# First sums of a two-layer graph network on one core: where two-piece float32r products begin, block 28 or block 21

## The chip, the cores and the metric

One core of a Trainium2 chip. The metric is the device time of one execution in microseconds (us), lower is better; the median of three executions of the kernel before is 3544.65 us.

## The reference, cut to what matters

6,250 nodes with 128 features, 200,000 edges sorted by destination. `h` is the layer norm of `x` followed by relu. Layer 0 (SAGE) needs for each node the mean of `h` over its incoming edges:

```python
msgs = h[src]
summed = jax.ops.segment_sum(msgs, dst, num_segments=N_NODES)
cnt = jax.ops.segment_sum(jnp.ones_like(dst, dtype=h.dtype), dst, num_segments=N_NODES)
return summed / jnp.maximum(cnt, 1.0)[:, None]
```

Two dense products, a residual and a layer norm follow; then comes layer 1, graph attention with four heads over the same edges, whose sums are done later in the kernel. Only the building of `summed` of layer 0 is touched here.

## The kernel before, in words

The kernel runs in stages one behind the other; `stage()` ends each with a barrier. The change concerns two of them.

**front** normalises `x` into `H`, finds where each node's edges start, and splits every row of `H` into pieces whose sum is the float32 value. The 49 blocks of 128 nodes are handled in seven groups of seven (`residual`, `lowest`, `second`, L487 to L668). Groups below `C_BF` = 28 become three bf16 pieces in `SPL`; the others become two pieces with 12 bits masked off, `CPR`, of type float32r. Between the groups ScalarE and TensorE also work through 26 steps of the edge attributes (`more(2)`).

**count_sums** computes the sums without fetching a row per edge. For each of 62 tiles (49 tiles of up to 128 edges per node, "pair tiles", and 13 tiles of the edges that did not fit, "odd tiles") it counts how often each source node occurs for each of 128 destinations, and multiplies this matrix of counts with the pieces of `H`. A tile of counts is made in eight units (u = 0 to 7) of 16 destinations:

- VectorE writes one-hot rows for two units at a time, `OHL` and `OHH` (`one_hots`, L1082), into a ring of three. It may start entry m when TensorE has used entry m-3 (`s_bm`). In an odd tile `OHL` is twice as long. It also adds up the pieces of a finished tile (`rows`, L1101) and prepares the next tiles' keys; its first one-hots of a tile need `LH`, which ScalarE turns at unit 2 of the tile before (L930).
- TensorE multiplies the one-hots of a unit into PSUM (`counts`, L981). `psA` has two places, so `counts` of unit n waits until unit n-2 has been copied.
- ScalarE copies each unit from PSUM into the bf16 matrix of counts `A[i % 2]` (L948).

The product of tile i-1 with the pieces is put between the counts of tile i: after `counts(i, u)`, for u of 1 and up, TensorE does `product(i - 1, range(7 * u - 7, 7 * u))`, seven blocks. A block h below `C_BF` takes the bf16 counts as weights and streams three pieces, 384 columns (L992). A block from `C_BF` on takes counts in float32r (`AR`) and streams two pieces, 256 columns (L998). ScalarE casts them, seven blocks a time (`cast`, L933 to L938), in the unit that `C_AT` names, behind that unit's copy:

```python
if u == 2 and i + 1 < NSL and of[i + 1] > of[i]:
    turned(of[i + 1])
if i >= 1 and u in C_AT:
    if u == C_AT[0]:
        act.wait_ge(s_ev, UNITS * i)
    cast(i - 1, C_AT.index(u))
```

So before the change block groups 28 to 34, 35 to 41 and 42 to 48 are multiplied in units 5, 6 and 7 and cast in units 1, 3 and 5. TensorE waits for cast g at the first block of its group (L997). The last tile has no tile behind it: all its casts and products are done at the end (L956 to L958 and the last call of `product`).

The order of the tiles is fixed: 14 pair tiles, then two pair tiles and two odd tiles in turn until the 13 odd ones are done, then pair tiles alone. GpSimd fetches the sources of each pair of tiles with an indirect DMA (L896), and ahead of that scatters 49 times into `s_tab` (L910), on which the edge lists of the odd tiles rest.

`OHH` and `AR` lie over tables that only later stages fill: `AR` begins at `tables_at`, and `OHH` behind its `C_FR` blocks.

Of the kernel before, what the change touches and what calls it, by code (L numbers as in the profile page):

```python
# [34 lines left out]
N_BLK = -(-N_NODES // P)  # L35
# [45 lines left out]
NV = N_BLK * P  # L81


C_BF, C_FR = 28, N_BLK - 28
C_CAST = [range(28, 35), range(35, 42), range(42, 49)]
C_AT = (1, 3, 5)
assert C_BF % 7 == 0 and C_FR == 7 * len(C_CAST)
PAST_ROW = 256.0
assert 2 * N_BLK <= P and PAST_ROW == 2 * P
# [51 lines left out]
def build(nc, x, src, dst, edge_attr, W1l, W1r, b1, W2l, W2r, b2, gamma, beta,  # L141
          W, W_edge, att_src, att_dst, att_edge, bias, out):
    with ExitStack() as top:
# [623 lines left out]
        def count_sums(at, block):  # L767
# [157 lines left out]
            def _(act):  # L925
                def turned(f):
                    act.wait_ge(s_tt, f + 1)
                    if f >= 2:
                        act.wait_ge(s_oh, UNITS // 2 * (last[f - 2] + 1))
                    act.copy(LH[:, f % 2], psT[:, 0:2 * P].rearrange("p (n c) -> p n c", n=2)[:, :, :, None]  # L930
                             .to_broadcast([P, 2, P, 2])).then_inc(s_lh, 1)

                def cast(i, g):  # L933
                    rows_ = C_CAST[g]
                    if i >= 1:
                        act.wait_ge(s_cu, len(C_CAST) * (i - 1) + g + 1)
                    act.copy(AR[:, rows_[0] - C_BF:rows_[-1] + 1 - C_BF], A[i % 2][:, rows_[0]:rows_[-1] + 1]
                             ).then_inc(s_cs, 1)  # L938

                turned(0)  # L940
                for i in range(NSL):
                    for u in range(UNITS):
                        n = UNITS * i + u
                        act.wait_ge(s_bm, n + 1)
                        if u == 0 and i >= 2:
                            act.wait_ge(s_cu, len(C_CAST) * (i - 1))
                            act.wait_ge(s_sv[i % 2], 16 * (i // 2))
                        act.copy(A[i % 2][:, :, UN_S * u:UN_S * (u + 1)].rearrange("p h (k s) -> p k h s", k=2),  # L948
                                 psA[:, n % 2, :, 0:W8].rearrange("p k (s h) -> p k h s", s=8)).then_inc(s_ev, 1)
# [6 lines that stand above are left out]
                act.wait_ge(s_ev, UNITS * NSL)  # L956
                for g in range(len(C_CAST)):
                    cast(NSL - 1, g)  # L958

            @block.tensor  # L960
            def _(pe):
# [23 lines left out]
                def product(i, rows):  # L985
# [4 lines left out]
                    for h in rows:  # L990
# [4 lines left out]
                        g = (h - C_BF) // 7  # L995
                        if h == C_CAST[g][0]:
                            pe.wait_ge(s_cs, len(C_CAST) * i + g + 1)  # L997
# [1631 lines left out]
```

## Time and profile before

| | before |
|---|---|
| runs (us) | 3544.65, 3550.16, 3542.03; median 3544.65 |
| the profiled execution | 3543.3 us, its span 3541.5 us |
| mean granted TensorE clock over the span | 0.803 |
| TensorE busy / its weight loads | 82% / 70% of the span |
| VectorE / ScalarE / GpSimd busy | 72% / 39% / 55% |
| stage count_sums | from about 125 us to 829 us of the span |

Start times in rows of the timeline are us from the start of the span. A timeline row merges neighbouring instructions of one line: `x7` are seven. The bracket at its end tells how long the engine had been idle before it and what released it. In rows of PEld (weight loads) a seven of L992 or L998 is one product of seven blocks, and the row of L981 before it is the counts of one unit (eight loads in a pair tile, sixteen in an odd one). A name such as `AE` for `A` is the profile's: the counts lie in the memory of tensor `AE`.

### The profile page before, as it was taken

The page shows a single profiled execution, that of the slowest core. Times are in us where ns is not written, and L with a number is a line of the kernel's source. Part 1 is how long each engine was busy: PE and PEld are TensorE (multiplying, and loading weights), DVE is VectorE, ACT ScalarE, POOL GpSimd, SP SyncE. Part 2 cuts the span into 40 slices and gives each one's busy share as a digit, 9 for nine tenths or more (in the row PEclk, how much of TensorE's full clock was granted, in tenths as well). Part 3 has the DMA queues.
Part 4 walks back from the last instruction along what each step waited for, and adds up shares of the span by engine and source line. Part 5 has one row for each costly group of instructions (what it writes and reads, how often), then busy time and mean ns, then how long its engine had stood idle before and what let it go on. Part 6 is the DMA issues. An engine that isn't in the chain of part 4 may idle for free. (4 is left out here: it accounts for less than half of the span.)

```text
span 3541.5 us, 66684 instructions
## 1 busy us (share of the span) xinstructions
PE 2894.2 (82%) x21816; PEld 2493.7 (70%) x21816; DVE 2558.1 (72%) x6864; ACT 1382.8 (39%) x2754; POOL 1941.0 (55%) x1972
## 2 busy tenths in 40 slices
PE   5789999999998999797777777777777777777774
PEld 5667777888877777587666766766666676676663
DVE  4779999995576765587666766766666676676667
ACT  4578777885445566322212222221221222222120
POOL 5430111251013332477777777777777777777773
PEclk9999999999999999676666666666666666666666
DMA  5233333582379888322222222222222222222225
GB/s 170 102 139 151 135 154 149 166 192 92 112 251 257 269 248 261 114 55 56 55 55 55 55 55 55 55 55 55 55 56 54 56 55 55 55 55 55 55 55 97
DMA packets 150470, 378.35 MB, mean 107 GB/s; under 512 B 39080, under 2 KB 87776, under 8 KB 141780
## 3 DMA queue, kind: packets, MB, share of 16 engines
q0 software_dynamic: 66640, 129.84, 17.4%
q1 hardware_dynamic: 42120, 217.23, 16.5%
q10 hardware_dynamic: 41372, 26.95, 2.6%
q8 instruction: 191, 3.13, 0.4%
q14 instruction: 147, 1.20, 0.1%
HBM read 255.78 MB, written 119.69 MB: 106 GB/s over the span
## 5 line engine op out<-in xcount | busy, mean ns | idle before, releaser
L2165 POOL DMA_INDIRECT G<-x_tab,idx x1611 | 1530.5, 950 | 490.8 <-issue 490.8
L2255 PE MATMUL pu<-MSG,OH 128*128 128x140 f32 x3282 | 627.0, 353 | 1.4 <-DVE ACC L2352 1.3
L2186 ACT COPY OHT<-pt 128x512 f32<-128x512 f32 (+1 forms) x432 | 236.5, 558 | 974.3 <-PE pt L2231 972.8
L2352 DVE TENSOR_TENSOR ACC<-pu,ACC 128x140 f32 x1641 | 485.1, 296 | 139.7 <-PE pu L2255 93.5
L2255 PEld LDWEIGHTS pu<-MSG,OH 128*128 128x128 f32 x3282 | 560.3, 247 | 4.8 <-DVE ACC L2352 1.4
L2244 PE MATMUL px<-ADG,OHT 128*128 128x4 f32 x3240 | 468.4, 271 | 0.0
L948 ACT CAST AE<-psA 128x784 bf16<-128x784 f32 x496 | 397.5, 815 | 139.2 <-PE psA L981 138.4
L2244 PEld LDWEIGHTS px<-ADG,OHT 128*128 128x128 f32 x3240 | 440.4, 213 | 10.4
L2277 PE MATMUL pc<-ident,L 128*60 128x128 f32 x108 | 42.3, 391 | 447.2 <-DVE L L2420 447.2
L1082 DVE TENSOR_TENSOR OHL<-iol,LH 128x2048 bf16<-128x2048 bf16 (+1 forms) x248 | 358.3, 1445 | 22.3 <-PE psA L981 16.2
L2231 PE MATMUL pt<-ident,OH 128*128 128x128 f32 x1620 | 354.9, 379 | 11.9 <-ACT OHT L2186 10.7
L2277 PEld LDWEIGHTS pc<-ident,L 128*60 128x60 f32 x108 | 13.6, 126 | 480.0 <-issue 480.0
L992 PE MATMUL psR<-SPL,AE 128*128 128x384 bf16 x1736 | 324.0, 327 | 0.0
L2231 PEld LDWEIGHTS pt<-ident,OH 128*128 128x128 f32 x1620 | 281.5, 200 | 60.2 <-ACT OHT L2186 35.1
L1627 ACT CAST AR<-AE 128x896 fp32r<-128x896 bf16 x248 | 246.0, 1017 | 163.8 <-PE psR L1816 107.8
L1816 PE MATMUL psR<-SPR,AR 128*128 128x256 f32 x1922 | 291.2, 297 | 15.2 <-ACT AR L1627 15.0
L2413 DVE TENSOR_TENSOR L<-G,AE 128x60 f32<-128x60 f32 x108 | 27.9, 258 | 350.4 <-DMA G<-x_tab,idx 350.3
L981 PE MATMUL psA<-OHH_c,OHL 128*128 128x98 bf16 (+1 forms) x4800 | 259.8, 201 | 22.9 <-DVE OHH_c L1082 22.5
L1816 PEld LDWEIGHTS psR<-SPR,AR 128*128 128x128 f32 x1922 | 253.0, 194 | 29.7 <-ACT AR L1627 20.0
L981 PEld LDWEIGHTS psA<-OHH_c,OHL 128*128 128x128 bf16 x4800 | 219.1, 98 | 71.6 <-DVE OHH_c L1082 35.6
L896 POOL DMA_INDIRECT srows<-src_pad,EKI x38 | 65.7, 1729 | 350.7 <-DVE KB L1064 194.5
L2323 DVE TENSOR_TENSOR MSG<-G,pq 128x1920 f32<-128x1920 f32 (+1 forms) x109 | 231.6, 2125 | 17.3 <-issue 17.3
(427 smaller groups left out, 4532.6 us busy)
## 6 DMA issues: line engine op xcount, KB each, us to landing
a_tab<-AE SPq DMA_DIRECT2D x62, 1568.0 KB, 5.7
AE<-a_tab SPq DMA_DIRECT2D x60, 800.0 KB, 5.6
AE<-a_tab SPq DMA_DIRECT2D x60, 768.0 KB, 7.0
G<-x_tab,idx POOLq DMA_INDIRECT x1611
at_in<-in_edge_attr SPq DMA_DIRECT2D x26, 250.0 KB
SUMS<-in_edge_attr ACTq DMA_DIRECT2D x24, 250.0 KB
ae_t<-room ACTq DMA_DIRECT2D x13, 256.0 KB, 7.0
AE<-ae_t SPq DMA_DIRECT2D x1, 3328.0 KB, 11.9
```

What stands on the lines that cost most here:

```text
L948: act.copy(A[i % 2][:, :, UN_S * u:UN_S * (u + 1)].rearrange("p h (k s) -> p k h s", k=2), psA[:, n % 2, :, 0:W8].rearrange("p k (s h) -> ...
L981: mm = pe.matmul(psA[:, n % 2, c * w // W8, to:to + w], OHL[:, m % RING, k], OHH[:, m % RING, k * step:k * step + w], start=True, stop=True)
L992: pe.matmul(psR[:, i % 2, 0:3 * D], A[i % 2][:, h, :], SPL[:, h].rearrange("p s f -> p (s f)"), start=(h == 0), stop=False)
L1082: return dve.tensor_tensor(out.rearrange("p (s h t) -> p s h t", s=k, t=2), columns[:, 0:w].rearrange("p (h t) -> p h t", t=2)[:, None].to ...
L1627: act.copy(AR[:, n % 3, 0:len(rows_)], A[i % 2][:, rows_[0]:rows_[-1] + 1]).then_inc(s_cs, 1)
L1816: mm = pe.matmul(psR[:, i % 2, 0:2 * D], AR[:, n % 3, k], SPR[:, h - N_BF].rearrange("p s f -> p (s f)"), start=False, stop=(h == N_BLK - 1))
L2165: pool.indirect_dma_start(G[:, u % 4, j, :], None, x_tab, bass.IndirectOffsetOnAxis(ap=idx[:, u % 4, j:j + 1], axis=0)).then_inc(s_g[u % 4 ...
L2186: act.copy(OHT[:, 4 * n:4 * n + w, :].rearrange("p a b -> p (a b)"), pt[:, n % 2, 0:w * P]).then_inc(s_te, 1)
L2231: mm = pe.transpose(pt[:, n % 2, (j % 4) * P:(j % 4 + 1) * P], OH[:, u % 4, j, :], ident[:])
L2244: mm = pe.matmul(px_l[:, :, j], OHT[:, j, :], ADG[:, j, :], start=True, stop=True)
L2255: mm = pe.matmul(pu[:, k[0], k[1]:k[1] + MW], OH[:, u % 4, j, :], MSG[:, u % 2, j, :], start=True, stop=True)
L2352: dve.tensor_tensor(a, pu[:, k[0], k[1]:k[1] + MW][:, None, :], a, ALU.add).then_inc(s_c, 1)
```

## The change

Three constants. The fourth group of seven blocks, 21 to 27, goes from three bf16 pieces to two float32r pieces; it is multiplied in unit 4. There are four casts a tile instead of three, and they stand in units 1, 2, 4 and 6.

```diff
-C_BF, C_FR = 28, N_BLK - 28
-C_CAST = [range(28, 35), range(35, 42), range(42, 49)]
-C_AT = (1, 3, 5)
+C_BF, C_FR = 21, N_BLK - 21
+C_CAST = [range(21, 28), range(28, 35), range(35, 42), range(42, 49)]
+C_AT = (1, 2, 4, 6)
```

With `C_BF` and `C_FR` the sizes of `SPL`, `CPR` and `AR` change, and the place of `OHH`. In front, the group 21 to 27 is now split as groups 28 to 48 are: `residual` masks bits instead of subtracting, and the cast of L507 into `SPL` falls away.

## Rows read from the trace of the kernel before

**Rows 1.** Busy time by stretch: us, then PE, PEld, DVE, ACT, POOL, PEclk, DMA share, GB/s
```profile
225.00:301.00 76.00, 76.00 (x831) 61.16 (x830) 70.85 (x101) 62.89 (x82) 6.22 (x5) 1.00 0.38 154
330.00:600.00 270.00, 253.99 (x3416) 201.06 (x3412) 268.82 (x315) 209.85 (x272) 42.46 (x17) 1.00 0.37 145
610.00:820.00 210.00, 210.00 (x2342) 170.13 (x2340) 192.64 (x236) 180.73 (x236) 71.12 (x55) 1.00 0.67 173
```
**Rows 2.** Waits, 300 to 600 us: waiter, releaser, us in total, times, longest
```profile
PE psA L981 <- DVE OHH_c L1082: 17.0, 21, 1.8
DVE OHL L1082 <- PE psA L981: 0.4, 1, 0.4
```
**Rows 3.** Waits, 600 to 830 us
```profile
DVE OHL L1082 <- PE psA L981: 8.9, 16, 0.7
```
**Rows 4.** Timeline of the weight loads, one pair tile: start us, us, engine, line
```profile
708.53 0.74 PEld L981 LDWEIGHTS psA<-OHH_c,OHL 128*128 128x128 bf16 x16
...
713.24 0.53 PEld L981 LDWEIGHTS psA<-OHH_c,OHL 128*128 128x128 bf16 x8
...
714.73 0.53 PEld L981 LDWEIGHTS psA<-OHH_c,OHL 128*128 128x128 bf16 x8
...
716.15 0.39 PEld L981 LDWEIGHTS psA<-OHH_c,OHL 128*128 128x128 bf16 x8
...
717.43 0.38 PEld L981 LDWEIGHTS psA<-OHH_c,OHL 128*128 128x128 bf16 x8
717.76 0.89 PEld L998 LDWEIGHTS psR<-CPR,AR_c 128*128 128x128 f32 x7
718.69 0.75 PEld L981 LDWEIGHTS psA<-OHH_c,OHL 128*128 128x128 bf16 x16
```
**Rows 5.** Timeline of ScalarE in units 5 to 7 of the same tile
```profile
715.46 0.81 ACT L948 CAST AE<-psA 128x784 bf16<-128x784 f32 x1 [0.63 <-PE psA L981]
716.16 0.95 ACT L937 CAST AR_c<-AE 128x896 fp32r<-128x896 bf16 x1
717.00 0.81 ACT L948 CAST AE<-psA 128x784 bf16<-128x784 f32 x1
718.00 0.81 ACT L948 CAST AE<-psA 128x784 bf16<-128x784 f32 x1 [0.18 <-PE psA L981]
```
**Rows 6.** Timeline at the end of the stage, last copy and bf16 products
```profile
820.28 0.81 ACT L948 CAST AE<-psA 128x784 bf16<-128x784 f32 x1 [0.18 <-PE psA L981]
...
821.14 4.34 PEld L992 LDWEIGHTS psR<-SPL,AE 128*128 128x128 bf16 x28 [0.21 <-ACT AE L948]
```
**Rows 7.** Timeline of VectorE where the first stretch of the stage ends
```profile
214.24 0.24 DVE L1056 TENSOR_SCALAR lo_i<-srows 128x128 int32<-128x128 int32 x1 [14.88 <-DMA srows<-src_pad,EKI]
```
**Rows 8.** Timeline of VectorE, last one-hots ahead of the odd tiles
```profile
301.22 1.23 DVE L1082 TENSOR_TENSOR OHL<-iol,LH 128x2048 bf16<-128x2048 bf16 x1 [0.44 <-PE psA L981]
...
306.16 2.29 DVE L1082 TENSOR_TENSOR OHL<-iol,LH 128x4096 bf16<-128x4096 bf16 x1 [0.34 <-ACT LH L930]
```
**Rows 9.** Timeline among the odd tiles: a counts load and the one-hot that needs it
```profile
445.35 0.53 PEld L981 LDWEIGHTS psA<-OHH_c,OHL 128*128 128x128 bf16 x8
...
447.71 2.29 DVE L1082 TENSOR_TENSOR OHL<-iol,LH 128x4096 bf16<-128x4096 bf16 x1
```
**Rows 10.** Timeline of the weight loads, last wait for one-hots in the stage
```profile
603.12 0.47 PEld L981 LDWEIGHTS psA<-OHH_c,OHL 128*128 128x128 bf16 x16 [0.73 <-DVE OHH_c L1082]
```
**Rows 11.** VectorE's sums of finished tiles, grouped by line, 228 to 304 us
```profile
L1101 DVE TENSOR_REDUCE SUMS<-psR 128x128 f32<-128x384 f32 x8 | 4.4, 547 | 0.0
```
**Rows 12.** The same, 606 to 822 us
```profile
L1101 DVE TENSOR_REDUCE SUMS<-psR 128x128 f32<-128x384 f32 x21 | 11.6, 552 | 6.5 <-PE psR L998 6.5
L1101 DVE TENSOR_REDUCE R<-psR 128x128 f32<-128x384 f32 x1 | 0.5, 549 | 0.0
```
**Rows 13.** Timeline of VectorE in front, the lowest pieces of blocks 21 to 27
```profile
91.39 1.09 DVE L665 TENSOR_TENSOR SPL<-SUMS,SPL 128x896 bf16<-128x896 f32 x1 [2.50 <-ACT SPL L490]
```

**Rows 14.** Weight loads of this line, 300 to 600 us: busy us, mean ns of one
```profile
L998 PEld LDWEIGHTS psR<-CPR,AR_c 128*128 128x128 f32 x538 | 68.8, 189 | 0.0
```

## The prediction

> **What bounds the kernel now.** I read the busy time by stretch first, since the change acts only while the first sums are built (about 130 to 829 us) and a little before. In the pair tiles ahead of and behind the odd ones TensorE is busy 76.00 of 76 us and 210.00 of 210; between 330 and 600 us it is VectorE, 268.82 of 270 [rows 1]. The waits say the same from the other side: among the odd tiles TensorE waits 17.0 us for one-hots, in 21 waits, and VectorE 0.4 us for TensorE [rows 2]; behind them VectorE waits 8.9 us for TensorE [rows 3], and TensorE's last wait for one-hots is at 603 us [rows 10]. So a microsecond of TensorE counts in pair tiles and is covered among odd ones.
>
> The pace of a pair tile is in its weight loads. A tile takes 718.69 - 708.53 = 10.16 us. A unit whose counts and product both follow bf16 work takes 714.73 - 713.24 = 1.49 us, the unit in which float32r begins 716.15 - 714.73 = 1.42, and a unit after that (718.69 - 716.15) / 2 = 1.27 [rows 4].
>
> Beside it runs ScalarE. It starts a copy 718.00 - 717.43 = 0.57 us after the first load of the counts (behind a float32r group), a cast 716.16 - 715.46 = 0.70 us after the copy, the next copy 717.00 - 716.16 = 0.84 us after the cast, and the cast takes 0.95 [rows 4, 5]. From the end of a copy to the load that waited for it pass 821.14 - (820.28 + 0.81) = 0.05 us [rows 6]. No row shows TensorE waiting for a cast of this stage now.
>
> **The change, part by part.**
>
> *Products.* Unit 4 turns from bf16 into float32r: one unit of 1.49 us goes, one of 1.27 comes, -0.22 us per pair tile.
>
> *The fourth cast.* Its duration isn't the question, its place is. Casts in units 1, 2 and 4 are early enough: the groups are needed in units 4, 5 and 6, and the tightest, cast in unit 4, ends about 0.73 + 0.70 + 0.95 = 2.4 us after the first load of that unit's counts (0.73 = 715.46 - 714.73), while its group is due two units later, after 1.42 + 1.27 + 0.33 = 3.0 us (0.33 from the counts' load to the group's, 717.76 - 717.43). The last cast stands in unit 6 and its group in unit 7. From the first load of unit 6's counts it can be there after 0.57 (copy may start) + 0.70 (cast starts) + 0.95 (cast done) + 0.05 (handed over) = 2.27 us. TensorE wants it after one unit and the counts of unit 7: 1.27 + 0.33 = 1.60 us [rows 4, 5, 6]. So TensorE waits 2.27 - 1.60 = 0.67 us in every tile. Before the change that cast stood a unit earlier and had 1.27 us more.
>
> Is ScalarE free by then? Behind the cast of unit 4 the copy of unit 5 starts at 0.73 + 0.70 + 0.84 = 2.27 us after unit 4's first load, instead of 1.42 + 0.57 = 1.99, and is over its 0.70 at 2.97; the copy of unit 6 can't start before 1.42 + 1.27 + 0.57 = 3.26. So the lateness does not add up. Its whole tile is 8 x 0.70 + 4 x 0.84 = 9.0 us and, every other tile, one turning of keys, under the new tile. What is queued behind the late cast is the copy of unit 7; it starts 0.57 + 0.70 + 0.84 = 2.11 us after unit 6's first load instead of 1.27 + 0.57 = 1.84, and the next counts come after the waiting product, later still. Nobody else waits for it.
>
> Net per pair tile in which TensorE sets the pace: +0.67 - 0.22 = **+0.45 us**, 10.61 for 10.16. VectorE's tile is at most 192.64 x 10.16 / 210 = 9.3 us of work there [rows 1], and stays covered.
>
> *How many tiles count.* Three parts:
> - Up to 214 us nothing: VectorE waits 14.88 us for an indirect DMA of sources, which stands on GpSimd behind its 49 scatters [rows 7]; the six or so tiles ahead of it, 0.45 us later each, fit into that.
> - From there to the odd tiles TensorE leads: 8 tiles are summed up between 228 and 304 us [rows 11]. The lateness goes over to VectorE by its last waits for TensorE's counts and for the turned keys, 0.44 us at 301.22 and 0.34 at 306.16 [rows 8]. 8 x 0.45 = +3.6 us.
> - Among the odd tiles VectorE leads. Does TensorE's lateness reach it through the ring of three? Two pair tiles in a row make TensorE at most 0.67 + 2 x 0.45 = 1.6 us late before VectorE's next long stretch. The tightest use that I find there: the one-hot at 447.71 needs counts loaded from 445.35, finished at about 445.35 + 0.73 = 446.1, 1.6 us before [rows 9]; at that point the lateness is 0.67 + 0.45 = 1.1 us. It holds, with 0.5 us to spare: 0 us.
> - After the last wait for one-hots at 603.12 [rows 10] TensorE leads to the end: 21 + 1 = 22 tiles [rows 12]. One of them carries the small merging products between counts and product of unit 6, which give the cast the time; I count 21: 21 x 0.45 = +9.4 us.
>
> *The end of the stage.* The last tile's products stand alone. Its seven blocks change their type too: -0.2 us as above. The 0.21 us that its first load waits for the last copy [rows 6] falls into the lateness: -0.2. The four casts run beside the first 21 blocks: these take 21 x 4.34 / 28 = 3.3 us, the cast needed first 0.95, each further one 0.84.
>
> *Front.* ScalarE loses one cast of seven blocks (0.95 us in count_sums [rows 5]), and the lowest piece of blocks 21 to 27 no longer waits 2.50 us for a copy of ScalarE's [rows 13]. The gain lies between 0 (the edge attributes' steps beside it are the pace) and 2.5 us. VectorE's next but one step waits for ScalarE's relu anyway, so only a part of that cast can come through: I take -0.5.
>
> Memory: the last table is written after the stage; no transfer is added. Each tile has one instruction more on ScalarE and one wait more on TensorE.
>
> **The sum.** 3.6 + 9.4 - 0.4 - 0.5 = +12.1 us. The profiled execution goes from 3543.3 to 3555.4 us. It lies 1.35 under the median of the runs, so in their terms 3544.65 + 12.1 = **3556.8 us**, 0.34% slower.
>
> **One rule against the trace.** Seven float32r loads are done within 0.89 us [rows 4] though one alone takes 189 ns [rows 14], which seven times over is 1.32: the loads overlap the matmuls and each other. The Trainium skill, "TensorE: Matmul & The Clock Gate", section "The mechanism", has it that a weight load overlaps matmuls in flight only when they use other rows of the array; by that rule the new group would cost its loads in full. The trace does not agree.
>
> **Rivals.**
> 1. *The wait isn't there and the saving is* (faster). TensorE would take up other work of its queue while the late group waits, the next tile's counts, so that only -0.22 is left. On 8 + 21 tiles that is -6.4, with -0.4 and -0.5 more about 3537 us. For it: all casts arrive in time now. Against it: the four durations above, and TensorE's waits for one-hots [rows 2], in which it did nothing else. It decides at 2.27 against 1.60 us. 7%.
> 2. *Covered* (no change). VectorE, 92% busy from 610 us on [rows 1], sets the pace more than I think, or the wait is 0.4 instead of 0.67: then +0.15 or so per tile, +4 us, 3549. For it: VectorE is close behind. Against it: it waits 16 times for TensorE [rows 3]. 11%.
> 3. *The odd tiles give way too* (slower still). If the 0.5 us to spare in the ring is less than nothing, each of the six rounds of two pair and two odd tiles loses up to 1 us: +6, 3563. 6%.
> 4. *The clock falls* (slower still). TensorE's waits of up to 1.8 us among the odd tiles leave the granted clock at 1.00 [rows 1, 2], that is 2.4 GHz, so 0.67 us a tile should too. If it spent 3% of 290 us at 1.2 GHz: about +9, 3565. The Trainium skill, "TensorE: Matmul & The Clock Gate", section "A second HAM failure mode: psum-queue depth-cycling", tells of frequent short idles between groups of matmuls that make the clock swing; the trace does not agree so far. 3%.
> 5. *Serial loads* (slower still). The new group's loads take 1.32 us instead of the 1.27 - 0.33 = 0.94 of its product now: +0.38 per tile, +11 us, 3568. Seven loads in 0.89 us speak against it. 1%. This is the rule of the section "The mechanism" as a mechanism.
>
> **How the numbers follow.** My forecast gets 72%: the wait rests on four measured durations, and the number of tiles on two counts. Its own range is 3549 to 3564 (0.35 to 0.55 net per tile, front 0 to -2.5, and the runs before spread from 3542 to 3550). A measurement of this kernel tells about 0.2%, 7 us, from no change, so slower means above 3551.7. Slower: forecast, 3, 4 and 5, 0.82. The same: 2, 0.11. Faster: 1, 0.07. The range of 3548 to 3565 takes in the forecast and rival 3.
>
> **What would show it.** In the profile after: a wait of the L998 loads for the cast of L937 of about 0.67 us, once a tile, in unit 7, up to 60 times (there is none now); tiles of 10.6 us behind the odd ones; four casts of 0.95 us; float32r sevens at 0.89; rounds of tiles among the odd ones as long as before; the wait at 214 us shorter. Wrong would be tiles of 9.94 us (rival 1), or VectorE waiting among the odd tiles (rival 3).

## The result, and the profile after

| | before | after |
|---|---|---|
| median of the runs, us | 3546.22 (3542.03 to 3556.97, 7 runs) | 3562.20 (3557.37 to 3569.17, 7 runs) |
| profiled execution, us (span) | 3543.3 (3541.5) | 3560.56 (3558.7) |
| ratio after to before | | 1.0040, 95% interval 1.0027 to 1.0053 |

The change makes the kernel slower by 0.40%, 14 us (10 to 19); the two medians themselves lie 16.0 us apart. Forecast were +12.1 us and 3556.8 us; the range of 3548 to 3565 holds the median.

The wait that the forecast rests on is there. First the waits of TensorE for this cast over the whole program, then those of 300 to 600 us and of 600 to 830 us, in the kernel after (waiter, releaser, us in total, times, longest):

```profile
PEld psR L998 <- ACT AR_c L937: 30.7, 61, 0.6
```
```profile
PEld psA L981 <- DVE OHH_c L1082: 21.3, 22, 2.1
PE psA L981 <- DVE OHH_c L1082: 15.6, 17, 1.8
PEld psR L998 <- ACT AR_c L937: 9.6, 26, 0.6
DVE OHL L1082 <- PE psA L981: 0.4, 1, 0.4
```
```profile
DVE OHL L1082 <- PE psA L981: 11.5, 22, 0.7
DVE OHL L1082 <- ACT LH L930: 7.2, 9, 1.0
```

Before, L998 waited for no cast. Now it waits 61 times: once in each tile that has a product between its counts, 0.62 us in pair tiles that TensorE leads, 0.16 to 0.5 us among the odd ones. Among the odd tiles VectorE's waits for TensorE are as before (0.4 us, once [rows 2]); behind them they grew from 8.9 us in 16 to 11.5 in 22 [rows 3], and those for the turned keys from 2.3 to 7.2.

In one pair tile behind the odd ones, first the weight loads of units 4 to 7, then ScalarE beside them (start us, us, engine, line; to be held against [rows 4, 5]):

```profile
721.27 0.53 PEld L981 LDWEIGHTS psA<-OHH_c,OHL 128*128 128x128 bf16 x8
721.75 0.90 PEld L998 LDWEIGHTS psR<-CPR,AR_c 128*128 128x128 f32 x7
722.68 0.39 PEld L981 LDWEIGHTS psA<-OHH_c,OHL 128*128 128x128 bf16 x8
723.02 0.89 PEld L998 LDWEIGHTS psR<-CPR,AR_c 128*128 128x128 f32 x7
723.95 0.38 PEld L981 LDWEIGHTS psA<-OHH_c,OHL 128*128 128x128 bf16 x8
724.28 0.89 PEld L998 LDWEIGHTS psR<-CPR,AR_c 128*128 128x128 f32 x7
725.22 0.39 PEld L981 LDWEIGHTS psA<-OHH_c,OHL 128*128 128x128 bf16 x8
726.23 0.89 PEld L998 LDWEIGHTS psR<-CPR,AR_c 128*128 128x128 f32 x7 [0.62 <-ACT AR_c L937]
727.17 0.75 PEld L981 LDWEIGHTS psA<-OHH_c,OHL 128*128 128x128 bf16 x16
```
```profile
724.53 0.81 ACT L948 CAST AE<-psA 128x784 bf16<-128x784 f32 x1 [0.17 <-PE psA L981]
725.24 0.94 ACT L937 CAST AR_c<-AE 128x896 fp32r<-128x896 bf16 x1
726.08 0.82 ACT L948 CAST AE<-psA 128x784 bf16<-128x784 f32 x1
```

Units 5 and 6 take 1.27 us each (counts at 722.68, 723.95, 725.22), and in unit 7 the last group's loads stand still. Unit 6 starts at 723.95; its copy starts at 724.53, the cast at 725.24, ends at 726.18, and the load comes at 726.23: 2.28 us after the unit's start, where the forecast had 2.27. Of the 2.28 - 1.60 = 0.68 us the row shows 0.62 as idle; the rest is the overlap with the counts' loads that is lost (a group that doesn't wait starts 0.33 us after the counts' first load, while those loads take 0.38).

Over seventeen pair tiles behind the odd ones, a tile takes 10.68 us (sums of finished tiles, L1101, from 642.44 to 823.94) where it took 10.23 (638.21 to 812.14): +0.45, as forecast. The 10.16 of the prediction is one tile of that row, a little shorter than the mean.

VectorE's sums of finished tiles mark the stage's stretches, before and after:

```profile
219.35 0.55 DVE L1101 TENSOR_REDUCE SUMS<-psR 128x128 f32<-128x384 f32 x1
330.99 0.55 DVE L1101 TENSOR_REDUCE SUMS<-psR 128x128 f32<-128x384 f32 x1
599.42 0.55 DVE L1101 TENSOR_REDUCE SUMS<-psR 128x128 f32<-128x384 f32 x1
828.42 0.56 DVE L1101 TENSOR_REDUCE SUMS<-psR 128x128 f32<-128x384 f32 x1 [6.68 <-PE psR L998]
```
```profile
219.38 0.55 DVE L1101 TENSOR_REDUCE SUMS<-psR 128x128 f32<-128x384 f32 x1
334.45 0.55 DVE L1101 TENSOR_REDUCE SUMS<-psR 128x128 f32<-128x384 f32 x1
602.85 0.55 DVE L1101 TENSOR_REDUCE SUMS<-psR 128x128 f32<-128x384 f32 x1
840.89 0.56 DVE L1101 TENSOR_REDUCE SUMS<-psR 128x128 f32<-128x384 f32 x1 [6.23 <-PE psR L998]
```

| stretch | before | after | difference | forecast |
|---|---|---|---|---|
| from the gap for the sources to VectorE's lead | 111.64 | 115.07 | +3.43 | +3.6 |
| odd tiles in turn | 268.43 | 268.40 | 0 | 0 |
| to the last sum | 229.00 | 238.04 | +9.04 | +9.4 - 0.4 |
| together | 609.07 | 621.51 | +12.44 | +12.6 |

The granted clock was 1.00 in the windows of 225 to 300, 330 to 600 and 640 to 800 us, as before.

### The profile page after: what moved, and what is told of

It is laid out like the page before. It is cut to its first block and busy times, and to the rows that moved or that the text cites. A ratio compares the mean times of both kernels' runs of the same rounds, so it can differ in the third digit from the quotient of the medians.

```text
span 3558.7 us, 66745 instructions
## 1 busy us (share of the span) xinstructions
PE 2887.6 (81%) x21816; PEld 2508.1 (70%) x21816; DVE 2555.3 (72%) x6864; ACT 1426.0 (40%) x2815; POOL 1936.4 (54%) x1972
## 5 line engine op out<-in xcount | busy, mean ns | idle before, releaser
L2244 PEld LDWEIGHTS px<-ADG,OHT 128*128 128x128 f32 x3240 | 442.6, 214 | 10.4
L998 PE MATMUL psR<-CPR,AR_c 128*128 128x256 f32 x1736 | 267.4, 293 | 22.0 <-ACT AR_c L937 21.8
```

What stands on the lines that cost most here:

```text
L998: mm = pe.matmul(psR[:, i % 2, 0:2 * D], AR[:, h - C_BF], CPR[:, h - C_BF].rearrange("p s f -> p (s f)"), start=False, stop=(h == N_BLK - 1))
L2244: mm = pe.matmul(px_l[:, :, j], OHT[:, j, :], ADG[:, j, :], start=True, stop=True)
```

## The experiments

My theory: the time is lost at the place of the last cast, and the fourth float32r group by itself is worth 0.22 us a pair tile. The edits are against the kernel after unless they say otherwise. All of them are read by the same stretch, from the sum behind the gap at about 219 us to the last sum, which was 609.07 us before and 621.51 after.

### The last two casts one unit earlier each

```diff
-C_AT = (1, 2, 4, 6)
+C_AT = (1, 2, 3, 5)
```

> The change with its casts in units 1, 2, 3 and 5 instead of 1, 2, 4 and 6. Theory A (the place of the last cast costs): the wait of about 0.62 us a tile goes and only the cheaper unit is left, -0.22 us on 8 + 21 tiles and -0.4 at the end, so 6 to 7 us under the kernel before (ratio 0.998), tiles of about 10.0 us behind the odd ones. Rival B (the fourth cast costs as work of ScalarE, wherever it stands): as slow as the change, ratio 1.004. Rival C (float32r blocks cost TensorE more than bf16 ones): slower than before too, with sevens longer than 0.94 us.

Measured: 3538.97 us against 3547.11 of the kernel before in the same set, ratio 0.9976 (0.9964 to 0.9988). It beats both kernels. L998 waits for no cast. The seventeen tiles behind the odd ones take 10.02 us each (636.18 to 806.53). One pair tile, weight loads, then ScalarE:

```profile
741.48 0.89 PEld L998 LDWEIGHTS psR<-CPR,AR_c 128*128 128x128 f32 x7
742.41 0.38 PEld L981 LDWEIGHTS psA<-OHH_c,OHL 128*128 128x128 bf16 x8
742.74 0.89 PEld L998 LDWEIGHTS psR<-CPR,AR_c 128*128 128x128 f32 x7
743.68 0.38 PEld L981 LDWEIGHTS psA<-OHH_c,OHL 128*128 128x128 bf16 x8
744.01 0.89 PEld L998 LDWEIGHTS psR<-CPR,AR_c 128*128 128x128 f32 x7
```
```profile
738.91 0.97 ACT L937 CAST AR_c<-AE 128x896 fp32r<-128x896 bf16 x1
739.75 0.84 ACT L948 CAST AE<-psA 128x784 bf16<-128x784 f32 x1
740.45 0.98 ACT L937 CAST AR_c<-AE 128x896 fp32r<-128x896 bf16 x1
741.30 1.56 ACT L948 CAST AE<-psA 128x784 bf16<-128x784 f32 x2
742.70 1.00 ACT L937 CAST AR_c<-AE 128x896 fp32r<-128x896 bf16 x1
```

The last group is loaded at 744.01, 0.31 us after its cast ended at 743.70. ScalarE works in this part of the tile without a pause, but TensorE doesn't feel it: its busy time is 75.00 of 75 us and 159.94 of 160 in the windows of 225 to 300 and 640 to 800 us. The stretch takes 603.03 us (219.25 to 822.28), 6.0 less than before; 29 tiles at 0.22 are 6.4, and with the end of the stage 6.8 had been expected. So the change's first part is the gain that the forecast put into it, and the places of the casts turned it into a loss; the next run moves the last one alone.

### The last two casts in units 4 and 5

```diff
-C_AT = (1, 2, 4, 6)
+C_AT = (1, 2, 4, 5)
```

> The change with its casts in units 1, 2, 4 and 5. Theory A: the last cast ends about 3.97 us after the first load of unit 4's counts and is wanted at 4.29, so it is in time by 0.3 us: as fast as with casts in 1, 2, 3 and 5, 6 to 7 us under the kernel before. Rival B: two casts in neighbouring units of 1.27 us make ScalarE late and cost some tenths a tile, ratio 1.000 to 1.004. Rival C: slower than before.

Measured: 3542.61 us, ratio 0.9979 (0.9965 to 0.9993). No wait for a cast; the stretch takes 602.65 us (217.81 to 820.46). This is the single move from unit 6 to 5, with the other three casts where the change has them. It gives back 18.9 us of the stretch, 29 tiles at 0.65, which is the forecast's 0.67. The two placings can't be told apart in time.

### The kernel before with its last cast in unit 6

Against the kernel before:

```diff
-C_AT = (1, 3, 5)
+C_AT = (1, 3, 6)
```

> The kernel before with its three casts in units 1, 3 and 6 instead of 1, 3 and 5: no fourth cast, no further float32r block. Theory A: a wait of 0.62 to 0.67 us a tile and nothing saved, on 8 + 21 tiles: +18 to +19 us, ratio 1.005; nothing lost among the odd tiles (lateness 1.3 us against 1.6). Rivals B and C: nothing changes, ratio 1.000, since ScalarE's work and the blocks are the same.

Measured: 3569.52 us, ratio 1.0068 (1.0049 to 1.0087), about +24 us (17 to 31). Its stretch grew by 19.9 us (218.76 to 847.74 is 628.98), where 18 to 19 were expected; the 4 us more in the ratio are within its interval. Seventeen tiles take 10.90 us each (644.96 to 830.29), 0.67 more than before. The waits of 600 to 830 us in it:

```profile
DVE OHL L1082 <- PE psA L981: 15.6, 27, 0.7
PEld psR L998 <- ACT AR_c L937: 12.4, 21, 0.6
```

With three groups and no fourth cast the same wait is there, once a tile and 0.6 us long in these. So neither the number of casts nor ScalarE's load makes it; the place alone does. Wait without saving costs 19.9, saving without wait brings 6.0 to 6.4, both together 12.4: the parts add up to within 1.5 us.

### The last cast in unit 7

```diff
-C_AT = (1, 2, 4, 6)
+C_AT = (1, 2, 4, 7)
```

> The change with its casts in units 1, 2, 4 and 7, a unit later still. Theory A: the wait is 0.57 + 0.70 + 0.95 + 0.05 - 0.33 = 1.94 us a tile, net 1.72 on 29 tiles: +50 us; and now the lateness at the tightest one-hot among the odd tiles, 3.7 us, is over the 1.6 that it can hide, so VectorE waits there up to 2 us in each of six rounds: +50 to +62 us in all, ratio 1.014 to 1.018. If the slack among the odd tiles is larger than I read it: +50. Rivals B and C: as slow as the change, +14.

Measured: 3683.12 us, ratio 1.0377 (1.0352 to 1.0401): far above what the wait alone would give. The stretch takes 740.49 us (220.96 to 961.45), 131 more than before; VectorE no longer waits at the gap at 214 us. The wait has the length that was worked out; what comes behind it was not expected. Weight loads at the end of a pair tile, then TensorE's matmuls, then the busy time of the window and of a quiet one (us, PE, PEld, DVE, ACT, POOL, granted clock, DMA share, GB/s):

```profile
806.88 0.89 PEld L998 LDWEIGHTS psR<-CPR,AR_c 128*128 128x128 f32 x7 [1.89 <-ACT AR_c L937]
...
809.16 0.15 PEld L992 LDWEIGHTS psR<-SPL,AE 128*128 128x128 bf16 x1 [0.17 <-issue]
809.48 0.15 PEld L992 LDWEIGHTS psR<-SPL,AE 128*128 128x128 bf16 x1 [0.17 <-issue]
...
813.26 0.95 PEld L992 LDWEIGHTS psR<-SPL,AE 128*128 128x128 bf16 x7
```
```profile
806.89 1.10 PE L998 MATMUL psR<-CPR,AR_c 128*128 128x256 f32 x7 [1.74 <-ACT AR_c L937]
...
808.84 2.45 PE L992 MATMUL psR<-SPL,AE 128*128 128x384 bf16 x7
```
```profile
808.00:812.00 4.00, 4.00 (x35) 2.73 (x33) 2.67 (x3) 2.39 (x4) 3.39 (x3) 0.57 1.06 275
816.00:820.00 4.00, 2.80 (x36) 2.54 (x32) 3.72 (x4) 3.35 (x5) 0.74 (x1) 1.00 0.13 11
```

Between 808 and 812 us the granted clock is 0.57, that is 1.2 GHz for most of the window, and the loads start 0.32 us apart. Seven of them at 2.4 GHz are done in 0.95 us (813.26). Before the clock fell the engine had stood still for 1.74 us, as it does once in every tile. Seven tiles from 713.10 to 808.02 take 13.56 us each, 3.33 more than the 10.23 of before: 1.89 - 0.22 = 1.67 is the wait less the saving, and the other 1.66 is what the slow stretch costs.

The wait alone does not settle it, though. It stands in the last tiles of the stage as well, 1.89 us once a tile, and there the clock stays up:

```profile
848.00:960.00 112.00, 96.34 (x1048) 79.82 (x1047) 81.25 (x97) 89.66 (x116) 34.17 (x25) 1.00 0.63 152
```

Nine tiles from 847.20 to 954.66 take 11.94 us each, 1.71 more than 10.23: the wait less the saving, and nothing for the clock. What keeps it up there no run shows.

And the odd tiles give way here. VectorE's waits from 330 to 700 us:

```profile
DVE OHL L1082 <- PE psA L981: 37.8, 41, 2.2
```

It was 0.4 us, once, in both kernels [rows 2]. The lateness of TensorE is now over what the ring of three has to spare: the rounds of two pair and two odd tiles take 54 to 56 us instead of 47.05, and the stretch of the odd tiles 313.11 us (361.83 to 674.94) instead of 268.43. It is the prediction's rival 3, at a lateness that this change doesn't reach.

The Trainium skill, "TensorE: Matmul & The Clock Gate", section "A second HAM failure mode: psum-queue depth-cycling", tells of short idles between groups of matmuls that make the clock swing. With idles of 1.74 us once a tile this trace agrees up to 825 us, and not behind that; with idles of 0.5 us once a tile (the kernel after) it does not.

### Does the clock need the fourth group, too?

Two kernels ran on another chip, on which the program takes some 1180 us longer, the kernel before included (4728.19 us there). With float32r from block 35 on, which ran on both chips, this stage starts 44 us later there (170.4 for 126.7) and its last sum comes 79 us later (918.50 for 839.03); the rest of the time is lost behind it. Only comparisons within that set count. Against the kernel before:

```diff
-C_AT = (1, 3, 5)
+C_AT = (1, 3, 7)
```

> The kernel before with its casts in units 1, 3 and 7. If the clock is what I missed with the last cast in unit 7 of the change: waits of 1.9 us a tile, behind each a stretch of 3.4 us at 1.2 GHz that costs 1.7 us, so 3.6 us on each pair tile (13.8 instead of 10.2), granted clock 0.88 to 0.91 in the stage, rounds of two pair and two odd tiles of some 54 to 55 us instead of 47: +140 us, ratio 1.039 to 1.041. If the excess came with the fourth group or the cast of unit 4 beside it instead, and the wait costs only its own length: 1.9 us on 29 tiles and up to 2 us in each of six rounds, +55 to +67 us, ratio 1.016 to 1.019, clock 1.00.

Measured: 4882.88 us, ratio 1.0335 (1.0312 to 1.0358), that is +158 us. Its windows:

```profile
330.00:600.00 270.00, 234.65 (x2757) 186.58 (x2755) 225.66 (x270) 181.18 (x232) 30.52 (x16) 0.93 0.30 122
640.00:800.00 160.00, 140.13 (x1687) 111.10 (x1688) 134.10 (x155) 106.70 (x138) 17.17 (x7) 0.91 0.32 128
```

With three groups the clock falls as well, and the loss is nearer to the +140 of the theory with the clock than to the +55 to 67 without. So the fall needs neither the fourth group nor the cast of unit 4. The 18 us over the 140 can be found in the sums of finished tiles. On that chip the gap for the sources lies behind the sum of the second tile and not of the fifth, so three more tiles count, 3 x 3.6 = 11 us; and the odd tiles take 312.9 us (439.55 to 752.47), 44.5 more than before, where the forecast left them 140 - 29 x 3.6 = 36. From the gap to the last sum pass 807.04 us (259.38 to 1066.42), and in the next kernel, on the same chip, 657.00 (261.50 to 918.50); that one is 32 x 0.22 = 7 us slower than the kernel before, so the stretch grew by about 157 us of the 158.

### Float32r from block 35 on

The other direction: 14 blocks in float32r, two casts, the last still in unit 5.

```diff
-C_BF, C_FR = 21, N_BLK - 21
-C_CAST = [range(21, 28), range(28, 35), range(35, 42), range(42, 49)]
-C_AT = (1, 2, 4, 6)
+C_BF, C_FR = 35, N_BLK - 35
+C_CAST = [range(35, 42), range(42, 49)]
+C_AT = (3, 5)
```

> The other way: only blocks 35 to 48 in float32r, two casts in units 3 and 5, products in units 6 and 7; one float32r group fewer than the kernel before. Theory A: every cast is in time (no wait of an L998 load), and one unit of 1.27 us turns back into 1.49: +0.22 us on 8 + 21 tiles and +0.2 at the end, 6 to 7 us over the kernel before, ratio 1.0018; the stage from the 14 us gap to its end is 6 us longer. Rival B (a cast costs as work of ScalarE): a cast fewer makes it faster than before, by 12 us if one cast more costs that. Rival C (float32r costs TensorE more): faster too.

Measured on that other chip: 4741.68 us, ratio 1.0026 (1.0012 to 1.0040), with a single wait for a cast, 0.15 us just behind the gap, and pair tiles of 10.4 to 10.5 us. It ran again on a chip like that of the first sets, with a profile of the kernel before beside it:

> The kernel before once more, for its profile on the chip of this set. All theories: no difference from the kernel before; its tiles behind the odd ones are the measure for the next run: 10.2 us.

> Blocks 35 to 48 alone in float32r, two casts in units 3 and 5, again, since the first time it came out at twice what Theory A says (+12 us against 6 to 7) on a chip that was 1180 us slower in the later stages. Theory A: the stage from its sources gap to its end 6 to 7 us longer than the kernel before, tiles behind the odd ones 10.4 to 10.5 us, ratio 1.0018. Rivals B and C (a cast, or a float32r group, costs more than it gives): shorter stage, ratio under 1.

Measured: 3549.61 us for 3546.69 of the kernel before in the same set, ratio 1.0020 (1.0006 to 1.0035); the profiled execution of the kernel before took 3544.35. The stretch takes 609.33 us in the first (218.57 to 827.90), 615.74 in the second (223.29 to 839.03): +6.4. The float32r group adds or saves the same in both directions, 6.0 to 6.4 us for 29 tiles, with ScalarE loaded less or more. So what a group gives or costs shows on TensorE alone.

What wasn't tried: a fifth group (float32r from block 14 on). `OHH`, which lies behind `AR`, would then reach into `rowi`, a small table that is filled earlier and read later, so the two would have to be placed anew. ScalarE's round would be 8 x 0.70 + 5 x 0.84 = 9.8 us and every other tile a turning of keys (0.48 to the next instruction, 738.43 to 738.91 in the first experiment), against 10.23 - 2 x 0.22 = 9.8 of TensorE: whether the gain goes on is open.

## Why the prediction was right

*What bounds.* Right. TensorE was busy 75.00 of 75 us where the last cast was early enough, and each change of its work came through in full in the pair tiles ahead of and behind the odd ones. Among the odd ones it did not come through at all, up to the lateness of this change; with the last cast in unit 7 it did.

*The product, -0.22 a pair tile.* Right: -6.0 and -6.4 us over 29 tiles alone, and +6.4 the other way. Three groups in a row at 1.27 us a unit, seven loads in 0.89 us each, speak once more against the rule of the Trainium skill ("TensorE: Matmul & The Clock Gate", section "The mechanism") that loads overlap matmuls only with other rows of the array. The same section also names a background weight buffer, into which a load may go ahead of matmuls in flight; these traces agree with that, and can't show the buffer.

*The late cast, +0.67.* Right: 2.28 us for 2.27, and 29 x 0.65 when the cast is moved back. Four durations, read where the same instructions already stood, gave a wait that no row of before showed.

*The number of tiles, 8 and 21.* Right to within 0.2 us in both stretches (+3.43 for +3.6, +9.04 for +9.0). One tile behind the odd ones waits only 0.16 us instead of 0.62 (at 630 us), as the prediction had it for the one with the merging products.

*The end of the stage, -0.4.* Right: from the last sum but one to the last pass 6.79 us (834.10 to 840.89) for 7.24 (821.18 to 828.42).

*The odd tiles, 0.* Right: 268.40 us for 268.43. The spare of 0.5 us held; unit 7's cast, with a lateness far over it, shows that there is such a limit.

*Who else waits: nobody.* Right for the time, incomplete as a list. The turned keys, which ScalarE writes in unit 2, reach VectorE later: its waits for them grew by 4.9 us behind the odd tiles. TensorE set the pace there anyway, and they lie beside its lateness, as the +9.04 shows. One of them stands ahead of the odd tiles, 1.01 us where [rows 8] have 0.34 at 306.16:

```profile
309.62 2.29 DVE L1082 TENSOR_TENSOR OHL<-iol,LH 128x4096 bf16<-128x4096 bf16 x1 [1.01 <-ACT LH L930]
```

*Front, -0.5, and the gap.* Wrong, and by my own argument. The same wait of VectorE in the kernel after:

```profile
214.28 0.23 DVE L1056 TENSOR_SCALAR lo_i<-srows 128x128 int32<-128x128 int32 x1 [15.26 <-DMA srows<-src_pad,EKI]
```

I had it shorter; it is 0.38 us longer than 14.88 [rows 7]. Both ends have to be counted from the stage's start (VectorE's first instruction of it, L1154, at 124.77 before and 122.65 after). From there the last one-hots ahead of the gap start at 75.40 us for 73.62, so the tiles were late by 1.8 us, and this lateness the gap swallowed, as forecast. But the gap also ended later, 91.63 us behind the start for 89.47. GpSimd's scatters begin with the stage and ended 1.6 us earlier than before (206.63 for 208.22); then GpSimd waited 4.22 us for them to land, for 2.51 before, and the fetch behind them was issued at 211.74 for 211.61.

So the 2.1 us by which the stage began earlier were lost in this pair, and nothing of the -0.5 can be in the +12.44. That is no rule: over the seven profiled executions in which the gap ends between 212 and 219 us, it ends 89.4 to 91.6 us behind the stage's start, and the latest start, 126.70, has the latest end. This is the run with float32r from block 35 on:

```profile
218.20 0.23 DVE L1056 TENSOR_SCALAR lo_i<-srows 128x128 int32<-128x128 int32 x1 [16.07 <-DMA srows<-src_pad,EKI]
```

What moves the stage's start moves the gap's end too; the lateness of the tiles ahead does not. Nor can the 2.1 us be put down to the change: the stage starts at 123.2 to 124.8 us in three executions with block 28, at 122.7 to 124.7 in four with block 21, and at 126.7 in the one with block 35. Fewer blocks in float32r may start it later, but the first two overlap. Whether front gives the 0.5 us is open; in the sum of this pair it should have been 0.

*The sum.* The stretch grew by 12.44 us where 12.6 was forecast. The profiled execution took 17.2 us of span more, and the ratio says 14.2. Some 4.7 us of the profiled pair lie behind this stage, 1.8 of the ratio are not in the sum; nothing in those stages is touched, single executions spread by 12 to 15 us, and 12.4 is well inside the interval of 10 to 19. I leave it at that; no run shows a cause. The ratio's 14.2 and the forecast's 12.1 differ by 2.1 us: these 1.8, the 0.5 of front, less 0.2 in the stretch. That the whole program came out this close is in part luck, since single executions differ by more; that the stretch did is not.

*The rivals.* The stated range also takes in rival 2's 3549 us, so the profile tells it from the forecast and not the time alone. No wait: falls, 61 of them. Covered: falls, +9.04 in the stretch where VectorE was 92% busy. The odd tiles and the clock: fall for this change, and both are what happens one unit further on. Serial loads: falls, seven are done in 0.89 us as before.

## What to carry to other kernels

When work is moved to an engine with time to spare, its share of busy time says little; write down for each piece when its input is there, when its engine can start it, and when the consumer wants it. Here the same four casts cost nothing or 19 us by one number in a tuple, and moving the last cast alone one unit earlier turned a kernel 0.4% slower into one 0.21% faster. And a wait on another engine's chain (the gap at 214 us) swallows what is lost beside that chain, but follows whatever moves the chain's own start.

## What was not expected of the hardware

- Waits of 1.9 us once a tile cost about as much again through the clock in most tiles: granted clock 0.89, 0.91 and 0.88 in the windows of 225 to 300, 330 to 600 and 640 to 800 us with the last cast in unit 7, 0.57 just behind the wait, the next seven products in 2.45 us. In the last tiles of the same execution the same waits leave it at 1.00 (11.94 us a tile for 13.56). Waits of 0.6 us once a tile leave it at 1.00 everywhere, with three groups as with four, and so do waits of up to 1.8 us that come irregularly among the odd tiles. Where between 0.6 and 1.9 us it turns, and what else decides, wasn't measured.
- ScalarE kept copies and casts back to back for a stretch of the tile with each only 0.02 to 0.05 us longer than before (cast 0.97 to 1.00 for 0.95), so its intervals of 0.70 and 0.84 us hold under full load.
